# Six matmuls of constants ahead of the FFN's transposes, with the five engines' orders laid out anew

## What is computed

```python
x = x + _L0_attn_a_ref(_layernorm(x), w_q, w_k, w_v, w_o, gate, memories, memory_norms)
x = x + _L0_ffn_ref(_layernorm(x), W1, b1, W2, b2)
x = x + _L0_attn_b_ref(_layernorm(x), W_Q, W_K, W_V, W_O)
x = x + _L0_ffn_ref(_layernorm(x), W1, b1, W2, b2)

def _L0_ffn_ref(x, W1, b1, W2, b2):
    Wq1, Wq2 = _quantize(W1), _quantize(W2)      # weights of -1, 0 and 1
    h = relu(einsum('bsd,fd->bsf', x, Wq1) + b1)
    return einsum('bsf,df->bsd', h, Wq2) + b2
```

## Time and profile before

| | us |
|---|---|
| median of three runs | 2195.35 |
| the profiled execution | 2200.08 |
| its span, first to last instruction | 2198.2 |
| mean granted TensorE clock, share of full speed | 0.942 |

### The profile page before, as it was taken

The page is one execution under the profiler, slowest core; times in us unless marked ns, Lnnn a source line. Parts: engine busy times, 40 slices in busy tenths (PEclk is TensorE's granted clock), DMA queues, the critical chain, the costliest instruction groups (busy, mean ns, idle before and its releaser), DMA issues.

```text
span 2198.2 us, 47411 instructions
## 1 busy us (share of the span) xinstructions
PE 1885.9 (86%) x18306; PEld 1220.8 (56%) x18306; DVE 1500.7 (68%) x3612; ACT 1369.6 (62%) x2726; POOL 1190.9 (54%) x1280
## 2 busy tenths in 40 slices
PE   0356799999989898999999898999999898998886
PEld 0233456665656665665666655666656565665543
DVE  5545586877777686867777686867777676866351
ACT  0214376666768576666668576666668586765654
POOL 0235537375665748374665648374766658372422
PEclk9856899999999999999999999999999999999998
DMA  3101220303131221303031221303031222202020
GB/s 109 58 11 58 57 70 11 107 21 97 40 78 60 68 69 30 106 2 103 35 78 60 68 69 45 92 7 102 30 78 59 68 69 51 87 11 59 8 61 10
DMA packets 79248, 126.49 MB, mean 58 GB/s; under 512 B 13617, under 2 KB 65969, under 8 KB 74929
## 3 DMA queue, kind: packets, MB, share of 16 engines
q1 hardware_dynamic: 70576, 115.07, 18.9%
q10 hardware_dynamic: 8448, 8.39, 1.1%
HBM read 80.95 MB, written 42.47 MB: 56 GB/s over the span
## 4 chain that ended last, share of the span: by engine, by line
PE 50%; DVE 18%; ACT 11%; POOL 8%; DMA 7%; issue 3%; SPq 2%; POOLq 0%; ACTq 0%; DVEq 0%
PE bank L1428 10%; PE bank L1594 6%; PE bank L1567 5%; PE bank L1581 5%; PE bank L1415 4%; DMA qst<-by_dim 4%; DVE mxs L1283 3%; DVE place L1201 3%; ACT place L930 2%; POOL place L741 2%; POOL place L738 2%; PE bank L1392 2%; DVE stats L1068 2%; PE bank L1463 2%; PE bank L1569 2%
## 5 line engine op out<-in xcount | busy, mean ns | idle before, releaser
L1283 DVE TENSOR_REDUCE mxs<-bank 128x1 f32<-128x128 f32 (+3 forms) x1024 | 433.4, 482 | 120.5 <-PE bank L1569 118.9
L930 ACT ACTIVATE place<-bank 128x512 f32<-128x512 f32 (+1 forms) x768 | 349.3, 529 | 105.4 <-PE bank L1583 101.9
L667 POOL TENSOR_TENSOR place<-am,place 128x512 f16<-128x512 f32 x256 | 291.1, 1159 | 101.6 <-ACT place L832 101.6
L657 POOL TENSOR_TENSOR place<-place 128x512 f16<-128x512 f32 x256 | 301.6, 1186 | 66.4 <-ACT place L820 64.4
L1567 PE MATMUL bank<-kst,qst 96*128 96x128 f16 (+3 forms) x1024 | 252.3, 314 | 34.2 <-DMA qst<-by_dim 11.7
L1428 PE MATMUL bank<-w2q,place 128*128 128x256 f16 x2048 | 255.7, 275 | 1.8 <-POOL place L657 1.6
L1581 PE MATMUL bank<-qst,kst 128*128 128x512 f16 (+3 forms) x1024 | 232.6, 302 | 14.6 <-DVE mxs L1283 7.5
L1569 PE MATMUL bank<-mask_qk,identb 128*128 128x128 bf16 x1024 | 222.3, 226 | 0.0
L1428 PEld LDWEIGHTS bank<-w2q,place 128*128 128x128 f16 x2048 | 195.2, 99 | 39.9 <-issue 8.5
L817 ACT ACTIVATE place<-bank,b1c 128x512 f32<-128x512 f32 x256 | 174.5, 682 | 48.2 <-PE bank L1415 23.5
L832 ACT ACTIVATE place<-am 128x512 f16<-128x512 f32 x256 | 150.0, 627 | 85.4 <-DVE am L1127 85.4
(11 more groups left out here) (165 smaller groups left out, 4054.3 us busy)
## 6 DMA issues: line engine op xcount, KB each, us to landing
by_row<-place SPq DMA_DIRECT2D x128, 128.0 KB, 2.1
kst<-by_row SPq DMA_DIRECT2D x64, 256.0 KB, 3.3
qst<-by_row SPq DMA_DIRECT2D x32, 512.0 KB, 4.8
by_dim<-place SPq DMA_DIRECT2D x128, 128.0 KB, 2.9
kst<-by_dim SPq DMA_DIRECT2D x64, 256.0 KB, 4.3
qst<-by_dim SPq DMA_DIRECT2D x32, 512.0 KB, 6.3
xa<-x SPq DMA_DIRECT2D x16, 512.0 KB, 4.2
out<-xg ACTq DMA_DIRECT2D x16, 512.0 KB, 3.0
```

Of the source, the lines that this page charges most:

```text
L657: G.tensor_tensor(L.hl[:, m, :], L.hf[:, m % 2, :], L.hh[:, m, :], ALU.subtract).then_inc(s["hl"], 1)
L667: G.tensor_tensor(alp[:, n % 2, k, :], am[:, k, :], ahp[:, n % 2, k, :], ALU.subtract).then_inc(s["al"], 1)
L930: A.activation(pf[h % SLOTS][:, S2_COL[k]:S2_COL[k] + S2_W[k]], bank_of(L2, ("S2", h, k))[:, 0:S2_W[k]], ACT.Exp, scale=D ** -0.5 / RS ** ...
L1283: V.tensor_reduce(mxs[:, g:g + 1], bank_of(L2, ("S1", n, k))[:, Q_AT[i]:Q_AT[i] + (i + 1) * P], AX, ALU.max).then_inc(s["mx"], 1)
```

## The change

Both FFN lanes get a new step on TensorE, WM, ahead of their turn. It takes the turn's two banks, which the turn took before, and runs six matmuls of 128 x 512 from the resident weight tile `w1q` into them. Nothing reads what they write; the transposes write the banks over. So 192 matmuls are added in all, six in each of the 32 turns, and the wait for the two banks now stands ahead of them.

```diff
+WARM = 6
@@ turn @@
-                into = take_both(L, [("T", 0, k) for k in range(KH)], t)
+                into = [bank_of(L, ("T", 0, k)) for k in range(KH)] if L is F1 or L is F2 else take_both(
+                    L, [("T", 0, k) for k in range(KH)], t)
@@ ffn, on TensorE @@
+                yield mark("WM")
+                into = take_both(L, [("T", 0, k) for k in range(KH)], t)
+                for n in range(WARM):
+                    T.matmul(into[n % 2][:, :], w1q[:, 0, 0:P], w1q[:, n % 2, 0:S], start=True, stop=True)
                 yield mark("FTT")
                 turn(L, t)
@@ MARKS, lane 3 (F2), pe @@
-            "FTT": [7],
-            "UP": [13.7, 15.8, 16.7, 22.7, 24.9, 25.7, 27.9, 29.8],
+            "WM": [0],
+            "FTT": [14.5],
+            "UP": [20.1, 20.9, 24.4, 25.2, 26.4, 28.6, 29.4, 31],
...
```

More of the change, by code:

```diff
@@ L80 @@
         "sync": {
-            "T": [28.6],
-            "PA": [56.5, 69.4],
+            "T": [25.3],
+            "PA": [55.8, 85.6],
         },
         "pool": {
[L85 to L90, removed]
+            "N": [74.1, 78.3, 90.9, 98.8, 104.1, 111.1, 114.2, 6.3, 8.6, 27.2],
+            "NP": [74.2, 84.1, 93.1, 102.1, 108.6, 113.3, 117.3, 8.5, 17.2, 28.5],
+            "T": [34.8],
+            "PA": [0, 47.6, 49.4, 54.5, 57.9],
+            "RW": [71],
+            "ST": [72, 72.9],
         },
         "act": {
[L93 to L102, removed]
+            "N": [73.4, 77.6, 89.6, 98.1, 103.4, 107.4, 113, 2.5, 14.8, 18.9],
+            "NT": [75.6, 77.7, 90.6, 99.1, 105.5, 111.1, 119.3, 7.1, 15.9, 20.1],
+            "T": [36.2],
+            "TT": [38.7],
+            "PA": [44.3, 45.6, 48.2, 53.3, 57.2],
+            "SS": [57.7],
+            "V": [58.1, 58.6],
+            "SK": [64.6, 65.1, 68],
+            "RM": [70.7],
+            "ST": [70.8, 71.2],
         },
         "dve": {
[11 rows of a table removed]
[11 rows of a table added]
         },
         "pe": {
[11 rows of a table removed]
[11 rows of a table added]
         },
@@ L145 @@
[L145 to L149, removed]
+            "T": [3.7],
+            "TT": [6.1],
+            "PB": [10.9, 13, 16.1, 18.8],
+            "PH": [14.7, 17.3, 20.8, 23.8],
+            "V": [24.3, 24.8],
+            "NM": [39.7, 54.3, 68.5, 84.2],
+            "NS": [46.9, 50.1, 52, 55.4, 59.1, 62.9, 66.7, 72.1, 75.5, 80.1, 82.7, 84.4, 90.8, 92.8, 95.3, 96.8],
@@ L150 @@
+            "EV": [61.4, 77.1, 92.1, 100.7],
+            "OT": [104.5, 105],
         },
         "dve": {
[L152 to L160, removed]
+            "T": [0.1],
@@ L161 @@
+            "TT": [6.8],
+            "PB": [12, 15.1, 17.2, 20.2, 25.8],
+            "PL": [0, 15.8, 18.1, 25.2],
+            "N": [28.3, 31.9, 33.5, 35.1, 37.4, 42.9, 48, 51.1, 53.3, 57.1, 61.8, 65.7, 68, 72.9, 77.5, 81.6],
+            "NM": [40, 54.6, 68.8, 84.5],
+            "TP": [65.1, 81, 94.6, 102.5],
+            "OT": [105.3, 106.1],
+            "WO": [108.3, 110.9],
         },
         "pe": {
-            "TT": [4.6],
-            "PB": [10.4, 12, 14.5, 17.5],
-            "V": [20.1, 21.4],
@@ L166 @@
[L166 to L172, removed]
+            "TT": [4.3],
+            "PB": [8.1, 11.5, 13.2, 15.7],
@@ L173 @@
+            "V": [17, 18.3],
+            "N": [27.8, 30.3, 32.8, 34.2, 36.9, 42.1, 47.5, 50.4, 52.8, 56, 61.3, 64, 67.5, 72.4, 77, 80.8],
+            "NM": [37.6, 53.6, 68.2, 83.8],
+            "NS": [45.4, 49.6, 51.5, 55, 58.2, 62.5, 66.2, 71.7, 73.6, 79.6, 82.2, 84, 88.6, 92.3, 94.4, 96.3],
+            "PV": [59, 74.8, 89.7, 98.4],
+            "TP": [63.5, 80.4, 94, 101.8],
+            "OT": [103.5, 103.9],
+            "WO": [106.8, 109.1],
         },
@@ L176 @@
         "pool": {
[L177 to L179 removed]
+            "FT": [4.9],
+            "XB": [9.5, 23.3],
+            "UP": [24.5, 25.8, 27.1, 28.4, 29.7, 31, 32.3, 33.7],
         },
         "act": {
[L182 to L185, removed]
+            "FT": [7.3],
+            "FTT": [17.8],
+            "UP": [21.3, 22.6, 25.7, 27, 28.3, 29.6, 30.9, 32.2],
+            "END": [64.2],
         },
         "dve": {
[L188 to L190 removed]
+            "FT": [3],
+            "FTT": [18.7],
+            "DN": [42.3, 60],
         },
         "pe": {
[L193 to L196 removed]
+            "WM": [0],
+            "FTT": [14.5],
+            "UP": [20.1, 20.9, 24.4, 25.2, 26.4, 28.6, 29.4, 31],
+            "DN": [31.1, 38.6],
+            "DM": [31.9, 32.1, 32.3, 32.5, 33.5, 33.7, 34, 34.9],
         },
@@ L200 @@
         "pool": {
-            "FT": [51.5],
-            "XB": [77.8, 79.1],
-            "UP": [80.3, 83.6, 91.3, 98.5, 99.6, 102.9, 105, 106.1],
+            "FT": [65.3],
+            "XB": [80.6, 81.8],
+            "UP": [83, 87.1, 88.4, 89.7, 101, 106.4, 107.5, 109.9],
         },
         "act": {
-            "FT": [59.9],
-            "FTT": [68.7],
-            "UP": [77.9, 82, 83.2, 95.8, 97.7, 100, 102.5, 104.1],
+            "FT": [68.7],
+            "FTT": [74.5],
+            "UP": [81.4, 85.7, 87, 88.3, 94.1, 99.3, 102.2, 108.5],
         },
         "dve": {
-            "FT": [45.8],
-            "FTT": [74.1],
-            "DN": [114.1, 115.9],
+            "FT": [63.4],
+            "FTT": [75.1],
+            "DN": [114.4, 119],
         },
         "pe": {
-            "FTT": [64.8],
-            "UP": [76.9, 80.7, 81.6, 82.9, 93.6, 97.5, 100.8, 102],
-            "DN": [102.1, 112.3],
-            "DM": [103.3, 104.9, 106, 107.9, 108.1, 108.3, 108.5, 109.2],
+            "WM": [64.7],
+            "FTT": [70.3],
+            "UP": [78.7, 83, 85.9, 86.7, 87.7, 93.1, 97.1, 101],
+            "DN": [104, 115.3],
+            "DM": [104.3, 104.5, 104.8, 110.9, 111.1, 111.3, 111.5, 112.2],
         },
```

12 lines of the change are left out of this document (4 added, 8 removed), and 44 rows, old and new, of the table MARKS.

## The result

The changed kernel takes 2199.47 us (median of 12 runs, 2193.29 to 2204.21) beside 2194.75 us of the kernel before (12 runs, 2188.10 to 2198.34). The ratio is 1.0027, with a 95% interval of 1.0017 to 1.0038. So it is slower by 0.27%, some 6 us. The direction was as predicted and the time lies in the range, but the forecast of 2225 us had five times the loss: +1.3%.

What follows compares the result with a forecast made beforehand. It took PE as the bound, with two holes and two clock falls per iteration. Terms 1.3 + 0 + 1.3 - 0.5 = +2.1 us, times 14 = 29.4 us or 1.3%, gave 2225 us (chance 0.52), range 2193 to 2245.

Steps and rivals of the forecast that it cites:

- F1's six: Six matmuls of constants at F1's turn, in a packed stretch: nothing hides them, +1.3 us an iteration.
- F2's six: Six matmuls of constants at the iteration's turn, ahead of A's products: covered by PE's wait for DVE, price 0.
- The turn: Iteration's turn, F2's turn moved back: B's chain 1.3 us earlier, between 0.7 with the clock fall on its projections and 2.1 without.
- the rival of the bad turn: Fall at the turn lasts twice as long and F2's six delay A's products: +3.9 us an iteration, 2250 us, chance 0.12.
- B's first scores: PE's wait for `qst`: two UP blocks moved behind (1.7) plus load (0.9) less earlier chain (1.3), net +1.3 us.
- the second fall stays: Ahead of B's first scores the hole is as long as before, so the clock still falls there: 0; if gone, -1.5 us.
- the load's 0.9 us: Input load issued earlier shares DMA engines longer with the read of `qst`: 0.9 us, bounds 0 and 1.2.
- The V block: A block of V fills PE's 0.7 us wait for ACT after B's ninth scores: -0.5 us, bounds -0.7 and 0.
- The second stack on SP: A's second stack goes out behind B's last mask rows, landing 3.8 us before its reader starts: price 0.
- The rest of the order: All other moves of the new order: 0, with 1 us either way.
- only the second fall goes: Rival: the clock fall at B's first scores goes, 2.1 - 1.5 = +0.6 us an iteration, 2204 us, chance 0.15.
- the change does nothing: Rival: the six run wholly in waits and the order is neutral, 2195 us, chance 0.09.

Runs made afterwards that it cites:

- the order alone: The changed kernel with WARM = 0, so the new order and early bank wait without the 192 matmuls: 2197.09 us, ratio 1.0030 to the kernel before.

## Why the prediction was wrong in its size

Step by step, for one iteration:

- **F1's six, +1.3.** Mis-sized. They measured 0.2 in the traces and 0.3 to 0.5 in the medians, which falls of the clock move as well. I read "nothing hides them" from the stretch of before with 0.27 us idle in 59, but the new order had made a wait in just this place, for DVE's L1251. In the old order, with 59.3 us in place of 57.9, the price was right.
- **F2's six, 0.** Right, with the cover as worked out: DVE takes up A's products when its own work is done, and PE's wait for it shrinks from 2.4 to 1.4 us. What I left out is their effect on the fall, on its length and on how many iterations have one, 0.2 to 0.3% of the time.
- **The turn, -1.3.** The mechanism held, a fall on B's projections in most iterations. It is as long as in the rival of the bad turn and takes 1.5 us, where I had 1.4 and, by taking 1.3 out of 2.1, counted 0.8; but B's chain came earlier by 2.4 us, more than the 2.1 I allowed, and in four iterations of 13 there was no fall.
- **B's first scores, +1.3, and "the second fall stays".** This is the step that failed. I charged the two UP blocks 1.7 us for leaving PE's wait. Put back on PE, they cost 1.6 us: ahead of the scores each of them waits for its bank, and the scores, on which DVE and ACT depend, wait behind them. The second fall is gone in all 13 iterations. I had priced that at -1.5, which is too much: the two iterations of the kernel before without it reach B's first PV 63.6 us behind DN, most others 64.4 to 65.3, so it is nearer 1 us. And the load's 0.9 us isn't there. It goes out 3.00 us behind the read of `qst` (1119.54 to 1122.54), not much earlier than the 3.65 of before, PE waits 0.5 us for `qst`, and the page's median landing of this read is 6.3 us in both kernels.
- **The V block, -0.5.** Right as far as it can be read. Between the fourth scores and the first PV PE was idle 1.4 us in 26.8 before and is idle 0.5 us in 25.3 now, as means of the 13, and the waits for ACT ahead of scores are not among those of PE after.
- **The second stack on SP, 0.** Right: no wait for `by_row` appears.
- **The rest of the order, 0.** Mis-sized. From B's first PV to the end the new order takes 2.5 us longer without the six (60.4 us in the order alone, 57.9 on average before), which is the whole lead of the first half. The old order there wouldn't have kept it either: with it the same time is spent ahead of B's first PV. The row of the order alone:

```profile
1155.90:1216.30 60.40, 58.41 (x709) 38.20 (x709) 43.49 (x108) 43.77 (x91) 37.60 (x41) 1.00 0.17 56
```

Taken together: on average over the 13 iterations B's first PV starts 62.0 us behind the end of F1's DN, where it started 64.8 us behind it before. The forecast had +0.8 us up to here (1.3 - 0.5) and the trace has -2.7. From there to the end of DN it is 60.6 us in place of 57.9, where the forecast had +1.3 and the trace has +2.7, some 2.5 of it by the order. So two errors of opposite sign cancelled in part, 3.5 us too dear and 1.4 too cheap, and the 2.1 us forecast became none. That the sign came out right is luck: the loss is the order's, which I had at 0 in the second half, and not that of the steps I charged. The forecast's own range was also added up too narrow. With the load, the chain and the moves at their bounds an iteration comes to +0.2 to +3.5 us, which is 2198 to 2244 and not 2208 to 2242. Of the rivals, "only the second fall goes", 2204 us, was nearest in its mechanism; in time "the change does nothing", 2195, was as near. I gave the former 0.15 because I took the fall to depend on the length of PE's hole ahead of the scores, and took that hole to be as long as before.

The length of single gaps did not decide it either. In the change the longest wait of PE at the turn is 1.4 us, and the clock still falls there in nine of 13 iterations; with the two holes filled it doesn't fall at all. The Trainium skill, "TensorE: Matmul & The Clock Gate", section "Why this matters for your kernels", wants no idle gap over some 3 us. By these rows a kernel can stay far inside that and lose the clock.

Open is why the second fall went. It isn't F2's six (the order alone lacks it as well), nor the place of the two UP blocks (with these back it stays away). What remains is that PE's one wait of 2.1 us there, for ACT, has become shorter ones; no run separates this from the earlier start of B's chain. Nor is it gone for good in this order, as it comes back in one iteration of 13 with F2's six alone, in one with F1's alone and in three with eighteen and F1's six. Open too is what holds the period at 121.2 us once the clock is whole, on DVE or elsewhere.

## What to carry to other kernels

Fillers pay where they fit the waits of a place, and more in several of its holes than in one: with nothing in them the new order was at 1.0030, with F2's six at 1.0010, and with eighteen matmuls in them at 0.9940. Before pricing an added piece in full in a packed stretch, look whether the same edit made a wait there; before charging a block for leaving a wait, look whether the block itself waits, and who stands behind it. A lead gained in one half of a pipelined iteration counts only if the other engines can follow.

## What the runs showed of the hardware

The fall at the turn grew shorter or rarer with what PE did ahead of it. It lasted about 10 us in most iterations with the order alone, about 7 with six matmuls at its start, 7 or 3 with six ahead of the projection, 3 with twelve, and there was none with eighteen. It shows in some iterations of the same kernel and not in others, though PE's work and waits ahead of it are alike (the iterations from 852 and 973 us), which I had not expected. Two kernels differ in the same way: with the two UP blocks put back, PE's instructions and waits up to the fall are those of the change, and yet the clock falls at the turn in two of 13 iterations, where it falls in nine of the change. So something besides the work at this place decides, and no run here shows what. A single iteration says little on the clock, and a count over one profiled execution is no exact measure either.
